# The last rows of two tiles go to the shifted copy in one transfer of two runs instead of one transfer per tile

## What is computed

```python
def shift_token(t):
    t1, t2 = jnp.split(t, 2, axis=-1)
    t2 = jnp.pad(t2, ((0, 0), (1, 0), (0, 0)))[:, :-1]
    return jnp.concatenate([t1, t2], axis=-1)
...
    x = x + o @ wo
    h = shift_token(x)
    mu = h.mean(-1, keepdims=True)
    var = h.var(-1, keepdims=True)
    h = (h - mu) / jnp.sqrt(var + 1e-05) * lg + lb
    h = h @ w1 + b1
```

## Time and profile before

| | us |
|---|---|
| median of 3 runs | 3000.75 (2998.53 to 3004.02) |
| the profiled execution | 3003.69 |
| its span | 3001.9 |

### The profile page before, as it was taken

How to read it: one execution, slowest core, us unless ns; L and a number is a source line. 1 busy time by engine, 2 the same in 40 slices (tenths; PEclk the granted TensorE clock), 3 DMA queues, 4 the chain that set the end, 5 groups by cost and what they waited for, 6 DMA issues and landing times.

```text
span 3001.9 us, 63211 instructions
## 1 busy us (share of the span) xinstructions
PE 2734.4 (91%) x21452; PEld 1918.9 (64%) x21452; DVE 2489.0 (83%) x7195; ACT 1793.8 (60%) x4181; POOL 1343.1 (45%) x949
## 2 busy tenths in 40 slices
PE   2399998999899998899989999899998999899997
PEld 2167675676666676666756767567765667666675
DVE  3489888888889887898878988889887988889895
ACT  2147673577646776376754767457764677637674
POOL 1145443545335454455534544344543545435552
PEclk9799999999999999999999999999999999999999
DMA  5100001000000000000010000100000000000000
GB/s 157 34 2 6 7 5 36 3 6 4 22 21 5 5 7 24 15 5 5 8 30 9 6 4 8 36 3 5 5 22 20 5 5 7 24 15 5 5 8 18
DMA packets 57996, 46.29 MB, mean 15 GB/s; under 512 B 18466, under 2 KB 54988, under 8 KB 57556
## 3 DMA queue, kind: packets, MB, share of 16 engines
q1 hardware_dynamic: 53520, 35.14, 4.2%
q10 hardware_dynamic: 4164, 7.12, 0.7%
HBM read 25.42 MB, written 8.44 MB: 11 GB/s over the span
## 4 chain that ended last, share of the span: by engine, by line
PE 64%; DVE 12%; ACT 6%; POOL 5%; issue 5%; DMA 4%; DVEq 0%; ACTq 0%; POOLq 0%
PE ps L134 11%; PE ps L135 11%; PE ps L136 11%; PE ps L400 8%; PE ps L426 7%; PE ps L411 5%; PE ps L335 4%; DMA XS<-xu 4%; PE ps L386 2%; PE ps L354 2%; ACT ar_b L569 2%; PE ps L294 2%; DVE ar_b L796 2%; POOL small L907 1%; DVE ar_b L780 1%
## 5 line engine op out<-in xcount | busy, mean ns | idle before, releaser
L907 POOL TENSOR_TENSOR small<-small,neg_half 128x16 f32<-128x16 f32 x128 | 406.2, 3174 | 416.7 <-DVE small L743 414.9
L569 ACT ACTIVATE ar_b<-ar_b,small 128x256 f32<-128x256 f32 (+1 forms) x1024 | 492.9, 484 | 103.6 <-DVE small L780 100.9
L780 DVE CUSTOM_DVE_ANT_0 ar_b<-ps,mask_t,small 128x256 f32<-128x256 f32 (+1 forms) x1024 | 419.5, 462 | 28.3 <-PE ps L400 25.1
L911 POOL TENSOR_TENSOR ar_c<-ar_c 128x1024 f32<-128x1024 f32 x128 | 301.9, 2358 | 229.7 <-DVE ar_c L769 229.0
L796 DVE TENSOR_SCALAR ar_b<-ar_b,rsw 128x256 f32<-128x256 f32 (+1 forms) x1024 | 302.9, 359 | 9.2 <-DVE rsw L789 0.2
L242 POOL TENSOR_SCALAR stats<-stats 128x2 f32<-128x2 f32 x128 | 29.9, 234 | 596.5 <-DVE stats L828 259.0
L134 PE MATMUL ps<-wqkv_hi,ht_hi 128*128 128x512 f16 x768 | 292.0, 380 | 0.0
L135 PE MATMUL ps<-wqkv_lo,ht_hi 128*128 128x512 f16 x768 | 291.1, 379 | 0.0
L136 PE MATMUL ps<-wqkv_hi,ht_lo 128*128 128x512 f16 x768 | 291.1, 379 | 0.0
L400 PE MATMUL ps<-ar_a 64*128 64x128 f32 x3840 | 271.4, 285 | 15.6 <-ACT ar_a L559 15.6
L411 PE MATMUL ps<-id_f,ar_b 128*128 128x128 f32 x1920 | 269.9, 276 | 17.0 <-DVE ar_b L796 16.5
(11 more groups left out here) (170 smaller groups left out, 6669.2 us busy)
## 6 DMA issues: line engine op xcount, KB each, us to landing
xu<-in_L_attn_x_dram SPq DMA_DIRECT2D x32, 256.0 KB, 2.9
out_dram<-xu SPq DMA_DIRECT2D x64, 128.0 KB, 2.8
XS<-xu SPq DMA_DIRECT2D x128, 63.5 KB
ar_a<-in_L_ffn_wqkv_dram ACTq DMA_DIRECT2D x1, 3072.0 KB, 16.9
modb<-mod_rows SPq DMA_DIRECT2D x8, 384.0 KB, 5.5
XS<-xu SPq DMA_DIRECT2D x112, 0.5 KB
ar_a<-in_L_wmod_dram SPq DMA_DIRECT2D x1, 1536.0 KB, 7.6
xu<-in_L_ffn_w_dram SPq DMA_DIRECT2D x1, 1364.0 KB, 9.3
```

The source lines that it names most:

```text
L569: last = act.activation(pw, pw, ACT.Exp, bias=mnw[:, n % 2, h:h + 1], scale=-1.0, accum_out=smw[:, n % 2, h:h + 1])
L780: last = dve.tensor_tensor_reduce(out=PW[:, f, q, i, c:2 * P], in0=ps[:, bk, i * 256 + c:(i + 1) * 256], in1=mask_t[:, c:2 * P], scale=rin ...
L907: pool.tensor_tensor(rinv[:, n % 4, :], ssm[:, n % 2, :], neg_half[:, 0:16], ALU.pow).then_inc(s_rinv, 1)
L911: pool.tensor_tensor(M1[:, n % 2, :], M1[:, n % 2, :], M2, ALU.add).then_inc(s_add, 1)
```

## The change

The even tile's body no longer has a row behind it. Behind the odd tile's body, one transfer of two runs of 512 B carries the last rows of both tiles: that of tile w - 1 into row 0 of tile w, and that of tile w into row 0 of tile w + 1. For the last tile the second run has no use; XS is made one tile (512 B in each partition) longer to hold it. All three transfers of a pair (two bodies, one of two runs) add to that pair's own semaphore, so ls waits for three in every pair.

```diff
-        XS = sb("XS", [P, NT, P])
+        XS = sb("XS", [P, NT + 1, P])
...
                         sp.dma_start(XS[1:P, w, :], U[0:P - 1, w, P:DIM]).then_inc(s_xs[l * 4 + w // 2], 16)
-                        if w + 1 < NT:
-                            sp.dma_start(XS[0:1, w + 1, :], U[P - 1:P, w, P:DIM]).then_inc(s_xs[l * 4 + (w + 1) // 2], 16)
+                        if w % 2:
+                            sp.dma_start(XS[0:1, w:w + 2, :], U[P - 1:P, w - 1:w + 1, P:DIM]).then_inc(s_xs[l * 4 + w // 2], 16)
...
-                        dve.wait_ge(s_xs[l * 4 + p], 16 * (4 - (p == 0)) * (b + 1))
+                        dve.wait_ge(s_xs[l * 4 + p], 16 * 3 * (b + 1))
```

## The result

| | before | changed |
|---|---|---|
| median, us | 3000.57 (6 runs, 2998.53 to 3004.02) | 3011.48 (6 runs, 3008.47 to 3016.14) |
| profiled execution, us | 3003.69 | 3011.39 |
| its span, us | 3001.9 | 3009.7 |

The ratio is 1.0036 with a 95% interval of 1.0023 to 1.0049: the change costs 10.9 us. A later series on another occasion gave 3013.23 against 3002.28 us, 1.0038 (1.0026 to 1.0051). The forecast of 3001.0 us was 10.5 us too low. The range of 2996 to 3012 held the first median by 0.5 us; that of the later series lies outside it.

What follows compares the result with a forecast made beforehand. PE was taken to bound the kernel, with seams where it waits on transfers into XS. The terms 0.6 - 0.35 + 0.05 gave +0.3 us on the profiled 3003.69; the median, 2.94 lower, made it 3001.0 us, range 2996 to 3012.

Steps and rivals of the forecast that it cites:

- the sign that was named for being wrong: On the chain: more than 22 to 24 pieces over XS, or one longer than 5.4 us, would show the forecast wrong.
- What bounds the kernel, and what is removed: PE bounds it, with 32 DVE waits for XS, 38.9 us; removing the rows behind the bodies is worth nothing.
- The spare time: Four pairs without a DVE wait have some 0.26, 1.1, 0.05 and 0.35 us to spare, so they add 0.
- d: How much later the two runs land than the odd body in front of them: taken as 0.05 us.
- completion in turn: Rival: the two runs are confirmed only after the body, 0.45 us a wait; 3010.6 to 3020.7 us; chance 13%.
- Its threshold, 0.3 us: Delay per wait from which the slower completion rival decides, if the 20 waits on the chain pass it on.
- The skill's rule with 0.04 us: Two runs go on two DMA engines, one run behind the body: 0.04 us in place of 0.05.
- Where d ends up: 12 chain waits in layer 0, pairs 1 and 3, at 0.05 us: +0.6 us; layer 0's other 12 waits uncounted.
- The layer's end: Layer 1, pair 3: modb starts later, relief 0.10 us in seven batches, -0.35 us with the delay; last batch +0.05.
- the relaxed end: Rival at layer 1, pair 3: the whole 0.54 us excess goes in seven batches; 2997.2 us; chance 9%.
- the cut into single elements: Rival: the two runs become 256 packets, adding 3 to 6 us to a landing; beyond 3100 us; chance 2%.
- The slower side: Whole kernel: the time rises by more than 0.2% (6 us); chance 15%.

Runs made afterwards that it cites:

- e1: Kernel before with its single rows, but the odd tile's row counts for its own pair, so the statistics wait for it: 3010.47 us, 1.0027.
- e3: Changed kernel with the two-run transfer issued twice, the second into an unused place and also waited for: 3012.94 us, 1.0032 against the kernel before.
- e7: Changed kernel with the modb load at layer 1's end held back until pair 3's statistics are taken: 3007.46 us, 1.0018 against the kernel before.
- e11: Changed kernel again, unaltered, on the same chip as the two kernels with dummy matmuls: 3013.23 us, 1.0038 against the kernel before.
- e8: Kernel before, transfers untouched, with a dummy DVE write of about 0.16 us ahead of the statistics in 32 places: 3008.55 us, 1.0017.
- e9: Changed kernel with four dummy matmuls per batch where PE waits ahead of tile 6 of layer 1: 3011.97 us, 1.0034 against the kernel before.
- e10: Kernel before with four dummy matmuls per batch where PE waits ahead of tile 6 of layer 1: 3006.02 us, 1.0014.
- e4: Kernel before with each body of 127 rows split into two transfers of 112 and 15 rows: 2972.4 us, 0.9895.

## Why the prediction missed the time

That the range of 2996 to 3012 us held 3011.48 is luck. Its upper end took in the lower part of a rival that was priced with 0.45 us a wait, the later series lies outside it, and the sign that was named for being wrong came true: the chain has 32 pieces over XS, not 22 to 24. L823 starts 4.91 us after the odd body's issue, which is neither the 4.75 to 4.85 of the forecast nor the 5.2 of the rival.

*What bounds the kernel, and what is removed*: right. The 24 + 8 waits of before are there, and nothing was gained by the 48 transfers fewer. (A single row stood behind the odd body in 48 of the 64 places, not in 56, and the closest body comes 1.5 us behind an even row, not 1.6; neither changes the sum.)

*The spare time*: right for three of the four other pairs, wrong for pair 1 of layer 1. It had no 0.05 us to spare. In the kernel before, its statistics already start 0.02 us after the body's confirmation in all 8 batches, but DVE's idle time there is at most 0.05 us, and the table of waits counts only idle time over 0.15 us. So it is missing from the 32, and it passes the whole of d on. After the change the table shows 3 of its 8 waits.

*d*: this step failed. I took 0.05 us from the packets, and the packets did end as told. But a landing is the packets and their confirmation, and the confirmation behind another one comes 0.16 to 0.20 us after it (e1, e3). No view of before shows this, but the trace has it in the row's last signal. My rival "completion in turn" had the mechanism, with the whole gap of 0.45 us for the price; it measured 0.16. Its threshold, 0.3 us, was worked out without pair 2, pair 1 of layer 1 and the clock, and the loss came already below it. (The skill's rule with 0.04 us would have taken 0.2 us from the sum, not 0.1.)

*Where d ends up*: I counted pairs 1 and 3 of layer 0 by the chain. The steps show pairs 1 and 2 of layer 0 and pair 1 of layer 1, 24 places, 3.7 us. A chain names one of several paths that are nearly equally long; the eight pairs 2 were on none of its pieces and still pass everything on, and pair 3's own delay keeps it. With d = 0.16 my formula would have given 12 x 0.16 + 2 x 0.11 = 2.1 us for these places, and 0.6 us for pair 3 of layer 1, where the later starts make 1.6.

*The layer's end*: wrong in sign. I took a relief of 0.10 us for each of seven batches; in six batches the statistics start 0.15 to 0.35 us later (5.44 to 5.63 against 5.26 to 5.33), in one 0.26 sooner. e7 puts the price of this traffic in the changed kernel at about 5 us, clock included.

*The clock*: missing from the sum. Of the profiled 9.07 us, 5.3 are the later starts of the statistics and 3.7 are left for it; in e11 it is 5.8 and 3.7 of 9.5. e8 shows the effect without the transfers, e9 and e10 that the sparse stretch lets the clock fall at tile 6. What stays open is why the drop comes in nearly every batch of one kernel and in few of another with the same sparse stretch, and so how much of the 10.9 us another build would show. By e9 and e10 about 6 us belong to the delay; the rest of the medians' 10.9, some 4 to 5 us, is put down to the drops' place and number by what is left over, not by a run that has this delay and none of the added drops.

*Rivals*: the relaxed end and the cut into single elements did not happen. The slower side, which I gave 15%, did; of what the forecast put at 76%, 2997.5 to 3004.5 us, nothing did.

## What to carry over

A small transfer joined to the last one that a consumer waits for is not free because its packets are: price its confirmation, 0.16 us here, at every wait that DVE really stands in, also one too short for the table of waits, and not only at those that the chain names. Look first at how a transfer is spread: 127 rows on one DMA engine took 4.75 us, 112 and 15 rows at most 2.66, and that saved 31 us (the clock's part in it included), where moving the last rows about cost 11. Where a kernel has sparse stretches of PE, a shift of a few tenths can cost several microseconds through the clock, and the granted clock of each execution, beside its time, shows it.

## What was not expected of the hardware

- Transfers queued behind each other are confirmed in turn, some 0.18 us apart, where a share of the later one lies behind the earlier one on its DMA engine, though that share's packets take 0.03 us or less. Their other shares are confirmed earlier: 3.30 to 3.42 us for 15 of the row's 16 (kernel before). A consumer that waits for both starts after 4.93 us in e1, 4.91 in the changed kernel and 5.10 in e3, against 4.75.
- Issuing on SP takes 0.6 us, but mostly 0.94 to 0.97 for the transfer issued right behind a body of 127 rows, for one run cut in 16 pieces as for two whole runs; behind the 15 rows of e4 the row takes 0.55.
- The same program with the same data took from 3000.4 us at a mean granted clock of 0.987 to 3012.2 us at 0.982 (e8). A trace was kept of a slow execution alone, so where the clock fell in the others is not shown.
